# Sorted edges as two streams: 64-row spans whose products alternate between the two halves of the TensorE array, with one carry for both

## The reference, cut to what matters

```python
# layer 0: row of sums = [ sum of table[src] | sum of edge_attr_64 | number of edges ], one row for each dst
# layer 1: row of sums = sum of edge_weight * table[src]
x.at[dst].add(messages)          # 50000 edges, 3125 rows of 321 (layer 0) or 256 (layer 1) f32 values
```

## Time and profile before

| | us |
|---|---|
| median of 3 runs | 2467.38 (2465.85 to 2475.86) |
| span of the profiled execution | 2243.7 |
| what lies around the span (median less span) | 223.7 |
| stage of edge sums, layer 0: first gather to last gather | 71.5 to 590.0 |
| the same, layer 1 | 1243.6 to 1755.4 |
| POOL, PE, DVE, ACT busy | 1063.1, 1905.4, 1248.5, 603.1 |

### The profile page before, as it was taken

The page is one execution under the profiler, slowest core; times in us unless marked ns, Lnnn a source line. Parts: engine busy times, 40 slices in busy tenths (PEclk is TensorE's granted clock), DMA queues, the critical chain, the costliest instruction groups (busy, mean ns, idle before and its releaser), DMA issues. The chain is left out here.

```text
span 2243.7 us, 33217 instructions
## 1 busy us (share of the span) xinstructions
PE 1905.4 (85%) x10298; PEld 1559.0 (69%) x10299; DVE 1248.5 (56%) x3125; ACT 603.1 (27%) x1303; POOL 1063.1 (47%) x1063
## 2 busy tenths in 40 slices
PE   6599798888586899999984979899999766799976
PEld 4366676666363899999982667778878653688865
DVE  7533788777475444444448558735544385333346
ACT  0222343333342111211113311222222131233324
POOL 0576777777520222222220677777777200355432
PEclk9999999999886899999996989999999987899998
DMA  7554555555364101111005534434444408221224
GB/s 230 153 147 137 158 148 143 144 143 144 96 261 171 33 31 36 30 34 34 30 22 166 172 111 114 127 115 128 127 126 121 129 18 342 84 64 62 67 65 144
DMA packets 175992, 258.49 MB, mean 115 GB/s; under 512 B 74113, under 2 KB 139357, under 8 KB 173460
## 3 DMA queue, kind: packets, MB, share of 16 engines
q0 software_dynamic: 49344, 131.89, 20.5%
q1 hardware_dynamic: 114644, 113.45, 15.3%
q10 hardware_dynamic: 11904, 11.96, 1.7%
HBM read 203.27 MB, written 56.86 MB: 116 GB/s over the span
## 5 line engine op out<-in xcount | busy, mean ns | idle before, releaser
L576 POOL DMA_INDIRECT agg_message<-table,edges_src x784 | 785.2, 1002 | 384.4 <-issue 231.8
L631 PE MATMUL agg_partial<-agg_message,moe_up 128*128 128x321 f32 x784 | 241.2, 462 | 63.2 <-DMA agg_message<-table,edges_src 46.6
L2464 PEld LDWEIGHTS ex_p_h<-ex_xT,ex_own_up 128*128 128x128 f32 (+1 forms) x2464 | 280.0, 191 | 2.7 <-issue 1.4
L2464 PE MATMUL ex_p_h<-ex_xT,ex_own_up 128*128 128x128 f32 (+1 forms) x2464 | 280.7, 276 | 1.0 <-DVE ex_xT L2515 1.0
L631 PEld LDWEIGHTS agg_partial<-agg_message,moe_up 128*128 128x128 f32 x784 | 156.9, 203 | 139.0 <-issue 75.4
L2423 POOL DMA_INDIRECT ex_x<-moe_in,route_token_at x58 | 57.2, 987 | 309.9 <-PE ex_p_x L2454 240.7
L2519 DVE COPY ex_own_up<-moe_up 128x1280 f32 x114 | 100.6, 884 | 167.3 <-PE ex_p_h L2464 166.5
L631 PE MATMUL agg_partial<-agg_message,agg_onehot 128*128 128x256 f32 x784 | 185.0, 389 | 8.1 <-issue 4.1
L631 PEld LDWEIGHTS agg_partial<-agg_message,agg_onehot 128*128 128x128 f32 x784 | 151.5, 195 | 35.8 <-issue 11.1
L641 ACT COPY agg_span<-agg_partial 128x321 f32<-128x321 f32 (+1 forms) x112 | 44.9, 401 | 417.4 <-PE agg_partial L634 409.1
L2589 POOL DMA_INDIRECT ex_x<-moe_in,route_token_at x66 | 64.4, 975 | 173.1 <-PE ex_p_x L2620 93.3
(11 more groups left out here) (588 smaller groups left out, 3323.4 us busy)
## 6 DMA issues: line engine op xcount, KB each, us to landing
agg_message<-table,edges_src POOLq DMA_INDIRECT x784, 2.8
agg_message<-in_edge_rows SPq DMA_DIRECT2D x56, 224.0 KB, 4.2
moe_up<-in_f_w SPq DMA_DIRECT2D x8, 1386.0 KB, 21.7
sums<-agg_span SPq DMA_DIRECT2D x56, 160.5 KB
moe_up<-in_f_w SPq DMA_DIRECT2D x4, 2048.0 KB, 14.6
moe_down<-in_f_w SPq DMA_DIRECT2D x4, 2048.0 KB
sums<-agg_span SPq DMA_DIRECT2D x56, 128.0 KB
moe0b_down<-in_f_w SPq DMA_DIRECT2D x8, 768.0 KB
```

Source lines behind the costliest of these rows:

```text
L576: pool.indirect_dma_start(out=to[:, k * w:k * w + D], out_offset=None, in_=self.table, in_offset=bass.IndirectOffsetOnAxis(ap=self.edges.s ...
L631: mm = pe.matmul(to, hot[:, k * P:(k + 1) * P], msg[:, k * w:(k + 1) * w], start=(k == 0), stop=(g == 0 and k == GE - 1))
L2464: return pe.matmul(to, own_up[:, o:o + n], xT[:, k * D + c * P:k * D + (c + 1) * P], start=(c == 0), stop=(c == 1))
```

## The change

The 391 tiles that hold edges are cut into two streams, A (tiles 0 to 194) and B (the other 196). A group now has 3 tiles of A and 3 of B (`RUN` = 3, `GE` = 6); there are 66 groups, of which the last has a single tile of B and none of A. A run of 3 tiles must fit in 64 nodes (`W`). The products of A write partitions 0 to 63 of the bank and those of B 64 to 127, in the order A, B, A, B, A, B, with 64 columns of one-hot as weights. One carry of full width shifts both halves: `apart` and `step` are set so that no row of one half reaches the other. `store` writes the two halves of 64 rows by two DMAs, with two register loads.

The streams meet in nodes 640 to 895: there B has 2 spare tiles of rows in `sums` (27 tiles instead of 25, the spare rows of before included 27 as well), and `link` adds the two overlapping tiles on DVE after they are loaded back. Tiles and groups of the stages: `QKV_GROUPS` 15 to 18, `LAYER1_GROUPS` (0, 5, 20, 56) to (0, 6, 24, 66), `HB` 14 to 18 (22 steps instead of 28).

```diff
-GE = 7
-EG = -(-E // (GE * P))
+RUN = 3
+GE = 2 * RUN
+W = P // 2
+EF = -(-E // P)
+EG = -(-EF // GE)
+FIRST = (EF // RUN) // 2 * RUN
+FIRST_RUNS = FIRST // RUN
+LINK, OVER = 5, 2
+ST = 27
-QKV_GROUPS = 15
+QKV_GROUPS = 18
-LAYER1_GROUPS = (0, 5, 20, EG)
+LAYER1_GROUPS = (0, 6, 24, EG)
-HB = 14
+HB = 18
...
     def store(self, sp, g):
-        row_at = sp.value_load(self.edges.row_at[0:1, g:g + 1], min_val=0, max_val=SPILL)
+        halves = range(0 if g < FIRST_RUNS else 1, 2)
+        row_at = [sp.value_load(self.edges.row_at[0:1, 2 * g + h:2 * g + h + 1], min_val=0, max_val=SPILL) for h in halves]
...
-            sp.wait_ge(self.stored, g * 16)
-        sp.dma_start(self.sums[bass.ds(row_at, P), :], self.held(g)).then_inc(self.stored, 16)
+            sp.wait_ge(self.stored, g * 32)
+        for h, at_row in zip(halves, row_at):
+            sp.dma_start(self.sums[bass.ds(at_row, W), :], self.held(g)[h * W:(h + 1) * W, :]).then_inc(self.stored, 16)
...
     def mark(self, dve, g):
         if self.weighted:
-            for k in range(GE):
+            for k in self.tiles(g):
                 t = g * GE + k
-                ins = dve.tensor_scalar(hot[:, k * P:(k + 1) * P], e.node[:, :], e.rel[:, t:t + 1], e.weight[:, t:t + 1],
+                ins = dve.tensor_scalar(hot[:, k * W:(k + 1) * W], e.node[:, 0:W], e.rel[:, t:t + 1], e.weight[:, t:t + 1],
                                         ALU.is_equal, ALU.mult)
         else:
-            dve.tensor_tensor(hot.rearrange("p (k n) -> p k n", n=P), e.node[:, :].unsqueeze(1).to_broadcast([P, GE, P]),
-                              e.rel[:, g * GE:(g + 1) * GE].unsqueeze(2).to_broadcast([P, GE, P]), ALU.is_equal)\
+            dve.tensor_tensor(hot.rearrange("p (k n) -> p k n", n=W), e.node[:, 0:W].unsqueeze(1).to_broadcast([P, GE, W]),
+                              e.rel[:, g * GE:(g + 1) * GE].unsqueeze(2).to_broadcast([P, GE, W]), ALU.is_equal)\
                 .then_inc(self.marked, 1)
...
-        for k in range(GE):
-            mm = pe.matmul(to, hot[:, k * P:(k + 1) * P], msg[:, k * w:(k + 1) * w],
-                           start=(k == 0), stop=(g == 0 and k == GE - 1))
+        for k in sorted(tiles, key=lambda k: k % RUN):
+            h = k // RUN
+            mm = pe.matmul(self.partial[h * W:(h + 1) * W, 0:w], hot[:, k * W:(k + 1) * W], msg[:, k * w:(k + 1) * w],
+                           start=(k % RUN == 0), stop=(g == 0 and k % RUN == RUN - 1))
         if g:
-            mm = pe.matmul(to, self.slot_shift(g), self.held(g - 1), start=False, stop=True)
+            to = self.rows(g)
+            mm = pe.matmul(self.partial[to, 0:w], self.slot_shift(g)[:, to], self.held(g - 1), start=False, stop=True)
...
+def slots_of(g):
+    first = g * GT
+    return (first if first <= LINK else slot_of(first)), slot_of(first + GT - 1) + 1
+
+def link(dve, acc, width):
+
+    size = OVER * width
+    first = slot_of(LINK) * width
+    return dve.tensor_tensor(acc[:, first:first + size], acc[:, first:first + size], acc[:, LINK * width:LINK * width + size],
+                             ALU.add)
...
             dve.wait_ge(loaded[0], 16)
             norms(0, GT, 1)
 
+            dve.wait_ge(loaded[LINK // GT], 16)
+            link(dve, acc, AW).then_inc(linked, 1)
+            dve.wait_ge(linked, 1)
```

More of the change, by code:

```diff
@@ L158, in clear_sums @@
     width = sums.shape[1]
-    for t in range(0, ROWS // P, 9):
+    for t in range(0, ST, 9):
         eng.dma_start(flat[:, t:t + 9, :], const.zero[:, 0:width].unsqueeze(1).to_broadcast([P, 9, width])).then_inc(cleared, 16)
@@ L409, in _ @@
             pe.wait_ge(floated, 1)
-            pe.matmul(p_base[:, 0:EG], first[:, :], self.dst[:, :].rearrange("p (g k) -> p g k", k=GE)[:, :, 0],
+            pe.matmul(p_base[:, 0:2 * EG], first[:, :], self.dst[:, :].rearrange("p (r k) -> p r k", k=RUN)[:, :, 0],
                       start=True, stop=True).then_inc(based, 1)
@@ L556, in __init__, with tiles, rows @@
         self.gathered, self.featured = ([m.sem(f"{n}{k}") for k in range(ring)] for n in ("gathered", "featured"))
-        self.counting, self.marked, self.shifted, self.used, self.moved, self.stored, self.asked = (
-            m.sem(n) for n in ("counting", "marked", "shifted", "used", "moved", "stored", "asked"))
+        self.counting, self.marked, self.shifted, self.used, self.moved, self.stored = (
+            m.sem(n) for n in ("counting", "marked", "shifted", "used", "moved", "stored"))
+    def tiles(self, g):
+        first = range(RUN) if g < FIRST_RUNS else ()
+        return [*first, *(RUN + k for k in range(RUN) if FIRST + g * RUN + k < EF)]
+    def rows(self, g):
+        return slice(0 if g < FIRST_RUNS else W, P)
     def slot(self, buf, g, size):
@@ L619, in products @@
         pe.wait_ge(self.marked, g + 1)
-        pe.wait_ge(self.gathered[g % self.ring], (g // self.ring + 1) * GE * 16)
+        tiles = self.tiles(g)
+        pe.wait_ge(self.gathered[g % self.ring], (g // self.ring * GE + len(tiles)) * 16)
         if self.edge_rows is not None:
@@ L639, in move @@
         if g > 1:
-            act.wait_ge(self.stored, (g - 1) * 16)
-        act.copy(self.held(g), self.partial[:, 0:self.width]).then_inc(self.moved, 1)
+            act.wait_ge(self.stored, (g - 1) * 32)
+        of = self.rows(g)
+        act.copy(self.held(g)[of, :], self.partial[of, 0:self.width]).then_inc(self.moved, 1)
     def feed(self, sp, groups):
@@ L1113, in norms @@
             def norms(first, last, n):
-                c.step(ts(deg[:, first:last], counts[:, first:last], 1.0, None, ALU.max))
+                c.step(ts(deg[:, first:last], counts(first, last), 1.0, None, ALU.max))
                 dve.sem_inc(deg_ready, 1)
```

116 lines of the change are left out of this document (77 added, 39 removed).

## The result

The changed kernel takes **2492.34 us** (median of 4 runs, 2485.55 to 2493.67) beside 2467.47 of the kernel before: ratio 1.0115, interval 1.0073 to 1.0157, so it is slower by 25 us where 23 us less were forecast. 2492 also lies outside the range.

A forecast was written before the change was run, and what follows sets the result against it. POOL's issue of indirect DMAs, 1.25 us a gather, was taken to bound both edge sums, with PE just under it. Terms of -17.3 us in layer 0 and -5.6 in layer 1 gave -23: 2444 us, range 2424 to 2476.

The forecast's parts named there:

- The step that failed: Whole kernel: profiled span 2243.7 us, median 2467.4; the 223.7 between left as is, span differences taken as median differences.
- the floor of both stages: Edge sums of both layers: POOL starts a gather each 1.25 us, 391 make 488.8 us, filling 94 and 96%.
- Its own criterion: Sign that the whole forecast is wrong: POOL's waits for PE grow past 20 us.
- Stores: Second store DMA and register load on SP per group: costs nothing, up to 2 us at the two tails.
- Marks: One-hots of half the width on DVE lengthen gathers less: 12 us gained in layer 0, 1 in layer 1.
- POOL's waits for products: Layer 0: waits in the qkv stage go, the mixer's may grow with the shorter ring; net gain 2 us.
- Products: Edge sums: halves overlap, saving about 155 us of PE work, worth nothing but the waits removed.
- Rivals A and B: A (0.18): the halves do not overlap, 2463 us. B (0.10): weight loads come into the open, slower, 2540 us.
- Change of width: PE between half and full width: 0.1 us each, 132 changes, 13 us of PE work a layer, hidden behind POOL.
- The tails: End of each layer's edge sum, after the last gather: the smaller last group gains 4 us in layer 0, 3 in layer 1.
- Clock (rival C): Mixer: PE less busy, granted clock falls from 0.95, priced at +12 from the forecast, 2456 us; chance 0.12.

The follow-up runs named there:

- kind II: Not a change: chips, or a condition, on which the kernel before takes 2446 to 2464 us; the result's chip is like these.
- kind I: Not a change: chips, or a condition, on which the kernel before takes 2245 us and the changed kernel 2231 (ratio 0.9935 and 0.9930).

## Why the prediction was wrong, point by point

**The step that failed** is its first: "the median 2467.4 lies 223.7 above, which I leave as it is, so a difference in the span is one in the median". The 223.7 us did not lie around the span. On kind II the edge sums take 221 us more (86 in layer 0, 135 in layer 1), and the runs were made where the sums' chain, and not POOL's issue, sets the end. A hint stood in its own table: 224 us around a span, where every later profile shows 2. With this the statement that POOL's issue of indirect DMAs is the floor of both stages was true of the profile and not of the runs. Its own criterion said so: POOL's waits past 20 us. Measured on the result's chip, without the waits for the table, 110 in layer 0 (49.9 by name, 60.0 of unknown sender) and 127 in layer 1 (86.2 by name, 40.7 put down to a DMA of the experts that had long been done).

**Stores: "SP works in the shadow", "Nothing".** This is the term that turned the sign. On kind II the second store and its row load cost 42 us, and this alone turns -14 into +25; cutting the store of the kernel before in two cost 23. On kind I no run varied the stores alone; that the changed kernel gains 15 us there with two stores agrees with a price near nothing. No rival had it. The view that it needed, a chain with late signals, was not in the profile.

**Marks, -12.** Right on kind I: 11 us, with a mean of 977 ns for "near 970". On kind II they are worth 18. The stage lost another 5.9 us on kind I by the one gather that escaped DVE's series, which the prediction had behind its last gather and so in the tail; POOL's waits for products fell by 3.5 us (8.4 to 4.9) for 2 forecast.

**Products.** The halves do overlap: 12 records in 1.84 us are 0.153 each for 0.16 forecast, and in layer 1

```profile
1500.62 1.51 PE L668 MATMUL agg_partial<-agg_message,agg_onehot 128*64 128x256 f32 x12
1502.07 0.70 PE L672 MATMUL agg_partial<-agg_span,agg_shift 128*128 128x256 f32 x2
```

0.126 for 0.13. PE's busy time fell by 112 us (1906.4 to 1794.6) for 150. Costing that at nothing was right on kind I; undoing part of the overlap moved nothing. Rivals A and B are out. The sentence of the Trainium skill (TensorE: Matmul & The Clock Gate, Part 3) that a load overlaps only with another row group is not borne out here: both halves use all rows, and 12 products with their loads took 1.84 us.

**Change of width, 0.1 us each, hidden.** Right but for a gap that it left out, and one row misleads. The carry's weight load waits 0.49 us for nothing that the trace shows (kind I):

```profile
581.71 0.30 PEld L672 LDWEIGHTS agg_partial<-agg_span,agg_shift 128*128 128x128 f32 x2 [0.49 <-issue]
```

But PE's products lose less. From the start of a full-width record to that of the first narrow one are 0.363 us, from the last narrow one to the carry's first 0.362, and on to its second 0.374 (medians in layer 0), where the kernel before has 0.269 each time. So a change costs 0.09 us, as forecast, and a third gap of 0.1 inside the carry comes on top: 0.3 us a group, 19 us of PE a layer for 13. It was hidden on kind I. That a change of the tiling mode drains the engine, as the Trainium skill says (TensorEngine Tiling (Array Packing), Key Properties), fits the first two gaps.

**The tails, -4 and -3.** Layer 0's went the other way. From last gather to last copy the changed kernel takes 18.8 us on kind I, the kernel before 11.2 (16.3 in the profile of the prediction, where the held gather was the last one). PE ends the last carry at 584.4; the copy that it releases starts at 596.39:

```profile
583.13 0.72 PE L668 MATMUL agg_partial<-agg_message,moe_up 128*64 128x321 f32 x2 [0.61 <-ACT agg_span L680]
583.69 0.70 PE L672 MATMUL agg_partial<-agg_span,agg_shift 128*64 128x321 f32 x2
```

```profile
595.85 0.42 ACT L1043 ACTIVATE mix_square<-layer_XN 128x256 f32<-128x256 f32 x1
596.17 0.19 ACT L1043 ACTIVATION_READ_ACCUMULATOR mix_square<-layer_XN 128x1 f32 x1
596.39 0.42 ACT L680 COPY agg_span<-agg_partial 64x321 f32<-64x321 f32 x1
```

The mixer's program puts the last group's copy behind 25 row norms on ACT (L1043, 0.54 us each, 13.5 us). Before, they ended at 603 and the products released the copy at 607.4. Now they are the end of the stage. So of the 19 us that the gathers gained, 11 reached the last copy (607.4 to 596.4). Layer 1's tail is 7.9 us for 8.9. Forecast of both tails -7, measured +6.6.

**Clock (rival C).** The mixer's granted clock fell from 0.93 to 0.86 on kind I, as the rival said, and cost nothing that shows. On kind II it stands lower still: 0.82 and 0.85 over the gathers of the two layers on the result's chip, with PE busy 66 and 73%, and 0.90 and 0.89 in the kernel before, with 78 and 80% (0.95 and 0.98 on kind I, 84 and 94%).

In sum: on kind I the forecast of -23 met -15 by the medians and -19 between the two profiles. Of these 19, layer 0's gathers gave 18.8 (15.3 forecast), layer 1's 6.0 (3.3), and the tails took 6.6 where 7 were to be gained. On kind II, where it was asked, the same terms were overrun by one that it had at zero.

## What to carry to other kernels

Compare the profile's span with the runs' time first: if they differ by more than a few us, the profile shows another execution than the one to be forecast, and the bound must be argued for both. A DMA issue that hides behind a longer step is only free if the signals around it are on time; a change that doubles the count of small DMAs should be tried on more than one chip. And when the work before a stage's end gets shorter, look at what stands ahead of the last step in its engine's program: here moving one copy (`edge_sums.move` of the last group) ahead of 25 row norms should give back up to 12 us. That was not tried.

## What the runs showed of the hardware

Two kinds of chip, or two conditions of one, 2245 and 2446 to 2467 us for the same program, at equal DMA packet times; nearly all of the difference lies in the edge sums. On the second kind, PE's signals reach ACT and DVE up to 8 us behind the end of its records in layer 0 and 12 in layer 1 (kernel before), and POOL 7 us behind it in the stretch shown, while signals of DVE and ACT arrive in 0.03 us. There SP's own instructions crawl at times: register and semaphore operations with medians of 17 to 42 ns take over 600, 96 such records in the changed kernel on the result's chip, 17 with one store, 12 in the kernel before, none in either kernel on kind I. The run without stores has none, but it has hardly any register operations left either (6 of 456), so it does not show that the crawl goes with the stores.

Products on the two column halves of the array run side by side at 0.153 us for 321 columns in float32 by their records, against 3.95 us for 14 records of full width. A change between full and half width cost PE 0.09 us, and the carry behind it another 0.1. A gather's issue on POOL lengthens under DVE instructions that run beside it: 1.54 us under a one-hot of 896 columns, 6.82 under a series of 25 SCALAR_TENSOR_TENSORs, for 0.95 alone.
